# The fp16 halves of a soft MoE's three weights made in earlier stages and kept in DRAM, and routed rows gathered as halves and transposed by DMA

## The reference

```python
x = x + tanh(g_xattn[0]) * conv(ctx, ctx, layernorm(x), ssm_kernel, D)   # causal convolution of head-wise outer products
x = x + tanh(g_ffn[0])   * moe(layernorm(x), ...)         # 8 routed experts, top 2, and a shared expert
x = x + tanh(g_xattn[1]) * linear_attention(layernorm(x), ctx, ...)      # 16 heads
x = x + tanh(g_ffn[1])   * soft_moe(layernorm(x), ...)    # 16 experts x 128 slots, hidden size 128

def soft_moe(x, gamma, beta, mu, scale, W1, b1, W2, b2):  # N = 256 tokens, D = 512, E = 16, S = 128
    x_ln = (x - mean) / sqrt(var + 1e-5) * gamma + beta
    logits = einsum('bnd,des->bnes', l2norm(x_ln, -1) * scale, l2norm(mu, 0))
    dispatch = softmax(logits, axis=1)                    # over tokens
    combine = softmax(logits.reshape(B, N, E * S), -1)    # over slots
    slot_in = einsum('bnd,bnes->besd', x_ln, dispatch)
    h = gelu(einsum('besd,edh->besh', slot_in, W1) + b1, exact)
    slot_out = einsum('besh,ehd->besd', h, W2) + b2
    return einsum('bsd,bns->bnd', slot_out, combine)
```

## Time and profile before

| | |
|---|---|
| median of 3 runs | 1921.48 us (1921.20 to 1922.18) |
| the profiled execution, its own time | 1924.44 us |
| its span in the profile | 1922.7 us |
| mean granted TensorE clock over the span | 0.937 of full speed |
| busy: PE, DVE, ACT, POOL | 1615.0 (84%), 1151.0 (60%), 735.9 (38%), 423.2 (22%) us |
| bytes moved by DMA | 168.08 MB, mean 87 GB/s |

### The profile page before, as it was taken

How to read it: one execution, slowest core, us unless ns; L and a number is a source line. 1 busy time by engine, 2 the same in 40 slices (tenths; PEclk the granted TensorE clock), 3 DMA queues, 4 the chain that set the end, 5 groups by cost and what they waited for, 6 DMA issues and landing times. The chain is left out here.

```text
span 1922.7 us, 28292 instructions
## 1 busy us (share of the span) xinstructions
PE 1615.0 (84%) x9752; PEld 950.1 (49%) x9753; DVE 1151.0 (60%) x2263; ACT 735.9 (38%) x1371; POOL 423.2 (22%) x318
## 2 busy tenths in 40 slices
PE   2989956999729999958888983676999999999997
PEld 2777742444316666624444542333555555555554
DVE  4988842333283333356876856576667676676654
ACT  2321103323232222224332421465656466565552
POOL 1333302223441111023313212153020110201000
PEclk9999977999959999978999996798999999999999
DMA  8222225233232222243113003343425143151432
GB/s 184 66 68 87 87 99 164 97 125 105 69 120 77 84 81 87 65 181 121 61 50 110 1 22 132 110 121 88 83 44 115 33 87 76 44 120 27 83 67 55
DMA packets 207631, 168.08 MB, mean 87 GB/s; under 512 B 141666, under 2 KB 158050, under 8 KB 207410
## 3 DMA queue, kind: packets, MB, share of 16 engines
q1 hardware_dynamic: 200384, 147.02, 27.6%
q0 software_dynamic: 5680, 18.62, 3.3%
q10 hardware_dynamic: 1474, 1.21, 0.3%
HBM read 101.98 MB, written 31.28 MB: 69 GB/s over the span
## 5 line engine op out<-in xcount | busy, mean ns | idle before, releaser
L1867 POOL TENSOR_TENSOR s_h_lo<-s_h,s_h_hi 128x512 f16<-128x512 f32 x32 | 37.0, 1155 | 517.1 <-DVE s_h_hi L2115 517.1
L2133 PE MATMUL s_ring<-w_mu_hi,s_xt_hi 128*128 128x512 f16 x256 | 100.5, 392 | 27.3 <-DVE s_xt_lo L2034 27.3
L274 POOL TENSOR_TENSOR prod_lo<-prod,prod_hi 128x2304 f16<-128x2304 f32 x16 | 73.3, 4580 | 166.2 <-ACT prod_hi L307 166.2
L463 PE MATMUL ring<-prod_hi,toep 128*128 128x288 f16 x320 | 92.2, 288 | 19.8 <-DVE terms L383 11.2
L2134 PE MATMUL s_ring<-w_mu_lo,s_xt_hi 128*128 128x512 f16 x256 | 100.4, 392 | 0.0
L2135 PE MATMUL s_ring<-w_mu_hi,s_xt_lo 128*128 128x512 f16 x256 | 100.0, 391 | 0.0
L2133 PE MATMUL s_ring<-w_w_hi,s_xt_hi 128*128 128x512 f16 x256 | 97.1, 379 | 2.1 <-issue 2.1
L2133 PE MATMUL s_acc<-w_w_hi,s_g_hi 128*128 128x512 f16 x256 | 97.2, 380 | 0.7 <-DVE s_g_lo L2118 0.3
L2135 PE MATMUL s_ring<-w_w_hi,s_xt_lo 128*128 128x512 f16 x256 | 97.1, 379 | 0.0
L2134 PE MATMUL s_ring<-w_w_lo,s_xt_hi 128*128 128x512 f16 x256 | 97.1, 379 | 0.0
L2135 PE MATMUL s_acc<-w_w_hi,s_g_lo 128*128 128x512 f16 x256 | 97.1, 379 | 0.0
(11 more groups left out here) (394 smaller groups left out, 4810.4 us busy)
## 6 DMA issues: line engine op xcount, KB each, us to landing
expert_rows<-e_y SPq DMA_DIRECT2D x39, 256.0 KB, 2.0
toep<-ssm_split SPq DMA_DIRECT2D x14, 512.0 KB, 5.1
stage<-in_L_ffn_gate_w SPq DMA_DIRECT2D x8, 704.0 KB, 7.2
stage<-in_L_ffn_up_w SPq DMA_DIRECT2D x8, 704.0 KB, 7.2
c_rows<-in_ctx SPq DMA_DIRECT2D x8, 512.0 KB, 10.7
x_rows<-in_x SPq DMA_DIRECT2D x8, 512.0 KB, 14.0
res<-in_x SPq DMA_DIRECT2D x128, 32.0 KB
after_conv<-gated SPq DMA_DIRECT2D x128, 32.0 KB
```

The costliest lines, as they stand in the source:

```text
L274: nc.gpsimd.tensor_tensor(prod_lo[:, u].rearrange("p k e r -> p (k e r)"), prod[:, u, :], prod_hi[:, u].rearrange("p k e r -> p (k e r)"), ...
L463: nc.tensor.matmul(out, w_hi, hi, start=(n == 0), stop=False)
L2133: mm(out_, a[0], b_[0], start=first, stop=False)
```

## The change

The halves of mu, W1 and W2 are no longer made in the soft MoE. Each is made in an earlier stage, and stored to DRAM as fp16 (`mu_split`, `w1_split`, `w2_split`, 4 quarters of 1 MB each): W1 in conv, one piece of 256 KB a step (hi on ACT, lo on POOL); W2 in shared, 16 pieces of 256 KB, four a chunk (hi on ACT, lo on DVE); mu in experts, four quarters of 1 MB, each spread over nine tiles in parts 0 to 8 (squares and root on ACT, sums, scaling and lo on POOL, sum over partitions and spread on PE, inverse on DVE). The soft MoE loads the halves, in twelve DMAs of 1 MB. Its `before` list loses the operations on weights, and the softmax part E of the turns 4 to 7 goes into the first batch's body, behind the first gelu. The first batch's LayerNorm gets a form of its own (`N2f`), in which DVE applies gamma and beta to one half of the rows and POOL to the other.

The other part is in the path of the routed rows. In shared they are split after they are normalised (hi on ACT, lo on DVE), and `normed_rows` holds halves, 2 KB a row as before; SP stores them at the end of the chunk. In experts SP transposes a gathered tile by DMA (`dma_start_transpose`, 8 blocks of 128x128 fp16), in place of PE's transposes and the split by ACT and DVE; POOL gathers as before. The expert stage's loop of 30 tiles is now written out.

The diff, cut to its core:

```diff
 conv_stage, sync:
             for s in range(STEPS):
                 if s + T_BUFS < STEPS:
                     load_toeplitz(s + T_BUFS)
+                if s == 0:
+                    for v in range(W1_BUFS):
+                        load_w1(v)
                 store(s)
                 if s + 2 < STEPS:
                     load_res(s + 2)
+                if s >= 2:
+                    store_w1(s - 2)
+                    if s - 2 + W1_BUFS < STEPS:
+                        load_w1(s - 2 + W1_BUFS)
+            for s in range(STEPS - 2, STEPS):
+                store_w1(s)
 conv_stage, gpsimd, in the loop over s, behind prod_lo:
+                if s >= 2:
+                    rest_of_w1(s - 2)      # w1_q lo = w1_in - w1_q hi
 conv_stage, scalar, in the loop over s:
                 if s + 2 < STEPS:
                     split(s + 2)
+                split_w1(s)                # w1_q hi = fp16(w1_in)
...
 shared_phase, sync:
             def chunk(c, u, last):
                 if not last:
                     load_x(c + 1, 1 - u)
-                sp.wait_ge(normed, (c + 1) * 4)
-                sp.dma_start(xn_d[:, bass.ds(c * 4, 4), :], xn[:, :, :]).then_inc(xn_stored, 16)
                 for q in range(4):
+                    if c * 4 + q >= 2:
+                        store_w2(c * 4 + q - 2)
+                    load_w2(c * 4 + q)
                     sp.wait_ge(ew_lo, c * 4 + (q + 1))
                     ...
                     sp.dma_start(stage[:, q % 2, :].rearrange("p (k i) -> p k i", k=KD), src).then_inc(stage_loaded[q % 2], 16)
+                sp.wait_ge(xq_hi_done, (c + 1) * 4)
+                sp.wait_ge(xq_lo_done, (c + 1) * 4)
+                sp.dma_start(xn_d[:, bass.ds(c * 4, 4), :], xq[:, :, :, :].rearrange("p t q d -> p t (q d)")).then_inc(xn_stored, 16)
 shared_phase, scalar:
                     if m < 4:
                         split_expert(c, m)
+                        nc.scalar.activation(xq[:, m, 0, :], xn[:, m, :], ACT.Copy).then_inc(xq_hi_done, 1)
+                        nc.scalar.activation(w2_q[:, v % 2, 0, :], w2_in[:, v % 2, :], ACT.Copy).then_inc(w2_hi, 1)
                     act.wait_ge(h_done, c * SK + (m + 3))
                     nc.scalar.activation(h_hi[0:r, m, :], h[0:r, u, :], ACT.Copy).then_inc(h_hi_done, 1)
 shared_phase, vector, behind h of block m:
+                    if m >= 1 and m < 5:
+                        nc.vector.tensor_tensor(xq[:, m - 1, 1, :], xn[:, m - 1, :], xq[:, m - 1, 0, :], ALU.subtract).then_inc(xq_lo_done, 1)
+                        nc.vector.tensor_tensor(w2_q[:, n % 2, 1, :], w2_in[:, n % 2, :], w2_q[:, n % 2, 0, :], ALU.subtract).then_inc(w2_lo, 1)
...
 expert_phase, tensor:
-                    for c in range(KD):
-                        last = nc.tensor.transpose(turn[:, c * P:(c + 1) * P], rows[:, u, c * P:(c + 1) * P], k.ident[:, :])
+            def quarter(j, part):
+                if part == 2:
+                    for e in range(JE):
+                        last = nc.tensor.matmul(mu_ps[:, e:e + 1], mu_square[:, 0, e * P:(e + 1) * P], ones[:, :], start=True, stop=True)
+                if part == 4:
+                    for e in range(JE):
+                        last = nc.tensor.matmul(mu_ps[:, e * P:(e + 1) * P], mu_inv[:, j, e:e + 1].to_broadcast([P, P]), k.ident[:, :], start=True, stop=True)
 expert_phase, scalar and vector:
-                    nc.scalar.activation(xt_hi[:, r % U, :], turn[:, :], ACT.Copy).then_inc(xt_hi_done, 1)
-                    nc.vector.tensor_tensor(xt_lo[:, r % U, :], turn[:, :], xt_hi[:, r % U, :], ALU.subtract).then_inc(xt_lo_done, 1)
 expert_phase, sync:
-            with sp.Fori(0, TILES // U) as i:
-                for u in range(U):
-                    sp.wait_ge(y_done, i * U + (u + 1))
-                    sp.dma_start(y_out[bass.ds((i * U + u) * P, P), :], y[:, u, :]).then_inc(stored[u], 16)
+            for n in range(TILES):
+                u = n % U
+                sp.wait_ge(gathered[u], (n // U + 1) * 16)
+                if n >= U:
+                    sp.wait_ge(expanded, n - U + 1)
+                sp.dma_start_transpose(xt[:, u], rows[:, u, :]).then_inc(turned[u], 16)
+                if n >= 3:
+                    store(n - 3)
+                if n < 2:
+                    load_mu(n)
+                if n >= SPAN + 3 and (n - 3) % SPAN == 0:
+                    j = (n - 3) // SPAN - 1
+                    store_mu(j)
+                    if j + 2 < NJ:
+                        load_mu(j + 2)
...
 soft_moe_phase:
-        before = (F1a + F1b + F2a + F2b + mu_ops(("MS", 0), ("MA", 0), ("MR", 0), ("MS", 1), ("BC", 0)) + ops("X", 0, 2, 1) + ...
-                  + late("L", 6) + split(5, 6) + late("L", 7) + N3a + N3b + softmax_in(0) + late("Z", 2) + split(6, 7) + softmax_in(1) + late("Z", 3) + split(7, 8)
-                  + softmax_in(2) + w2_split(0, 2) + late("Z", 4) + ... + w2_split(14, 16) + softmax_in(10) + E(6) + E(7))
+        before = (F1a + F1b + F2a + one("N2f", 0) + ops("X", 0, 2, 1) + F3a + F3b + ops("L", 0, 4, 1) + N1a + late("L", 4) + N1b + late("L", 5) + N2a + late("L", 6)
+                  + N2b + one("B2", 0) + late("L", 7) + late("Z", 0) + N3a + late("Z", 1) + N3b + softmax_in(0) + late("Z", 2) + softmax_in(1) + late("Z", 3)
+                  + softmax_in(2) + E(0) + late("Z", 4) + softmax_in(3) + E(1) + late("Z", 5) + softmax_in(4)
+                  + E(2) + late("Z", 6) + softmax_in(5) + E(3) + late("Z", 7) + softmax_in(6) + ... + softmax_in(10))
+        for op in body:
+            body0 += [op]
+            if op == (0, "HG", 0):
+                body0 += E0(4) + E0(5) + E0(6) + E0(7)
+                if op == "N2f":            # gpsimd: second half of the rows; vector does the same to x_ln[:, 0, :]
+                    nc.gpsimd.tensor_tensor(x_ln[:, 1, :], x_ln[:, 1, :], gam[:, :], ALU.mult).then_inc(S["x_gamma"], 1)
+                    nc.gpsimd.tensor_tensor(x_ln[:, 1, :], x_ln[:, 1, :], bet[:, :], ALU.add).then_inc(S["xln_done"], 1)
             for j in range(NJ):
-                sp.dma_start(mu_in[j], mu_d[:, :, j * D:(j + 1) * D]).then_inc(mu_loaded[j], 16)
+                sp.dma_start(w.mu[:, j].rearrange("p q k d -> p (q k d)"), mu_split[j]).then_inc(mu_in[j], 16)
             sp.dma_start(b2s[:, :], b2).then_inc(S["b2_loaded"], 16)
+            for j in range(NJ):
+                if j == 2:
+                    load_rows(1)
+                sp.dma_start(w.w1[:, j].rearrange("p q k d -> p (q k d)"), w1_split[j]).then_inc(w1_in[j], 16)
+            for j in range(NJ):
+                sp.dma_start(w.w2[:, j].rearrange("p q e d -> p (q e d)"), w2_split[j]).then_inc(w2_in[j], 16)
```

403 lines of the change are left out of this document (204 added, 199 removed).

## The result

The changed kernel took 1943.49 us in the median of four runs (1938.24 to 1951.22), the kernel before 1921.83 (1921.20 to 1922.48). The ratio, as the record works it out from the single runs and not from the two medians, is 1.0103, with a 95% interval of 1.0078 to 1.0127. That is slower by about 1%, clear of the noise, where faster was forecast (slower had a chance of 0.18), and outside the range. The profiled execution is the fastest of the four, 1938.24 us with a span of 1936.5. In the later rounds the kernel before took 1918.4 to 1930.4 us; two of its executions, of 7749.5 and 8150.8 us, count as slow and enter no ratio.

A forecast was written before the change was run, and what follows sets the result against it. PE was taken to bound experts and soft MoE batches, SP's loop conv, small-step order the soft MoE's start. Conv +15, shared +10, experts +8, soft MoE -49 sum to -16: 1908.4 profiled, forecast 1906 us median, range 1878 to 1932.

The forecast's parts named there:

- The soft MoE: Stretch ahead of the batches, where weights are no longer split: 49 us saved, batches unchanged.
- the stretch to G: Soft MoE, from the first D to the first G operation on PE: 14 us shorter than 63.0.
- DVE's two subtracts a block are hidden in its idle time: Shared: DVE's new subtracts cost nothing, as it is busy 76.3 of 227 us; stage forecast +10.
- The +22: Shared, upper bound: each new DVE subtract could wait for a POOL instruction of 2.86 and delay the next block's h.
- The loop: Conv: tile landing 5.1, step's work 9.2, store and residual issues 10.2 make two periods of 12.27, without slack.
- the 10 for the loop: Conv: W1's two DMAs ahead of the tile load add 1.7 a pass, in 6 iterations: +10 us.
- the 2 for the end: Conv's end: last stores and loads stand behind the rows' stores, some 5 issues: +2 us.
- the late transposes: Experts: mu's 1 MB DMAs delay the next transposes after tiles 12, 21 and 30, with slower PE clock: +14 us.
- Rival 1: Early stages' work hides: conv +5, shared +4, experts -5, soft MoE -49, total 1876 us; chance 0.20.
- rival 2: Experts: DMA transposes land late at every tile; at a landing of 6, +25 to 1931 us; chance 0.17.
- Rival 3: Soft MoE: softmax sets the start, gain 40 not 49, or first-body softmax delays: 1915 us; chance 0.17 with the like.
- rival 4: Soft MoE: first logits wait for halves because mu's loads come behind others; a few us at most, no separate chance.

The follow-up runs named there:

- w2_bufs: Changed kernel with four W2 buffers in shared, stage load issued first and W2's store three pieces late: shared 262.4 us, 13.6 below the changed kernel.
- no_mu: Changed kernel without any work on mu in the experts; the soft MoE loads W2's halves instead: experts 248.5 us, 28.1 less.
- w1_behind: Changed kernel with W1's store and load in conv issued right behind the Toeplitz load: that load lands in 7.3 us, period 13.5 to 13.6.

## Why the prediction was wrong

- **The soft MoE: right**, -49.8 for -49. D came 35.6 earlier for 34.5, the stretch to G is 16.9 shorter for 14, what follows 2.8 longer.
- **Shared: this step failed.** "DVE's two subtracts a block are hidden in its idle time." DVE had the time, but its instructions take 3.33 and 1.64, not 0.7, and SP waits for the second of them with the next stage load behind it in its queue. The prediction had listed what SP's queue gets, two issues, and not what the first of them waits for. It had also read the earlier trace rows wrongly: `s_dq`'s 1.25 at 1287.06 is no slower rate, but the rest of a POOL instruction of 1.15 that had begun at 1286.61, and 0.55 more; so beside one of 2.86 the subtract takes up to 3.4. By the Trainium skill ("SBUF — State Buffer", "Who interferes with whom") a DVE instruction with two SBUF inputs is blocked while POOL reads SBUF, which the prediction weighed and set aside. The trace agrees: 405.28 + 3.33 against POOL's end at 408.06. The +22 worked out by it is near the 23.9 measured, but by another path: it let the wait pass on through DVE's `h` of the next block, and w2_bufs, which leaves DVE's subtracts as they are and frees SP, takes 13.6 back. This step, from +10 to +23.9, is 14 of the 30 us between forecast and profiled time.
- **Conv: mechanism right, size off**, +21.3 for +15. The loop is as said: (5.9 + 9.2 + 10.2 + 1.5) / 2 = 13.4 is the period seen in its settled part, 1.1 more than before for the 0.9 forecast. Forecast for the whole were 10, 2 and 2; measured +16.6 at the last added rows and +4.7 behind them. The terms that were mis-sized are the 10 for the loop and the 2 for the end. The surplus is in the steps before the loop settles, two of 15.3 and 15.2 for 12.6 and 12.2 (the second with the clock at half from 147.2 to 150.6, for which the sum had no term), and in the end, where the last stores of W1 wait for their landings. The median lies 5 us above the profiled execution, which was taken to lie 3 above the median.
- **Experts: mechanism right, size off**, +18.1 for +8. The tile's gain (5.85 for 5.86) and PE's work on mu (0.85 a time for 0.92) are as said. The term that was mis-sized is the late transposes: the stalls are 19.1 (6.7, 8.8, 3.6) for 14, so they do wait for mu's bytes. Not counted was that mu's first two quarters load ahead of the second and third transposes: the first three periods are 20.1, in no_mu 14.9. Nor were the three late tiles away from mu's DMAs, 4.0 together. The end took 2.8 for 2.
- **The range** gave each term its upper end and then let the sum stay well below their sum (+31, +22, +30). All three missed the same way. In shared and at the start of the experts the cause is one: what is put in an in-order queue was priced by its own length, and not by what it waits for and what waits behind it. Conv missed the same way for causes of its own.
- Rival 1 (the work hides) is refuted by the three stages' losses, rival 2 (transposes late at every tile) by the period of 5.85 in 20 of 38 intervals; rival 2's sign was right for another reason. Rival 3 gave the soft MoE a gain of 40, measured 49.8. For rival 4 the first logits would have to wait for loads: they wait 0.65 for DVE's split instead, and start 18.0 after the stage, where the sum had 17.9.

## What to carry to other kernels

Price a DMA that is put in an in-order queue by the wait in front of it: which engine makes its data, what that engine is locked by, and what stands behind it in the queue. Give a by-product as many buffers as it needs to be stored without waiting. Bytes put beside a load on the critical loop cost it in whatever order they are issued (here in every order tried); make them where they cost least, as W1, which cost 19.6 in conv and 8.0 in the soft MoE.

## What the runs showed of the hardware

- A DVE subtract of two SBUF operands waits for the POOL instruction that is running: 3.33 us beside one of 2.86, 0.68 alone. It holds the other way too: POOL's subtract at 408.02, begun while DVE's ran, took 1.61 in place of 1.16.
- DMAs issued behind a load delay it: the Toeplitz load lands in 5.1 without W1's DMAs, in 7.3 with 512 KB issued right behind it and in 9.5 with the residual's loads from another engine's queue in flight. By the Trainium skill ("DMA: Bandwidth & Descriptors", "Queues, rings and completion order") a ring's descriptors are taken in order by each engine. The landings did come in the order of issue (215.25, 215.91 and 216.53 in w1_behind for the Toeplitz load and the two behind it), and the first was late all the same.
- The issue of a DMA transpose takes SP 1.2 to 1.3 us at least, and 3.66 behind a store and a load of 1 MB each; it lands 2.7 after its issue at the earliest, up to 6.3 in no_mu.
- In conv, steps at a granted clock of 1.00 take 9.1 us from PE's first matmul to the added rows, steps with a stretch at 0.50 in them 10.4 to 12.0.
